# Group statistics, diagonal marks, SiLU and two per-token columns rearranged in an attention and graph-convolution kernel

## The chip, the cores and the metric

The kernel runs on one core of a Trainium2 chip. The metric is device time in microseconds (us) of one execution. A kernel's time is given as the median of several runs; the profile comes from one further execution with its own time.

## The reference, cut to what matters

Input: x, 16 samples of 64 channels by 1024 tokens (32 x 32), f32. The reference applies two residual blocks:

```
y   = gn32(x)                          # 32 groups of 2 channels
q,k = w_q y, w_k y;  v = w_v y         # 4 heads of 32
q   = softmax over 32 dims * scale;  k = softmax over 1024 tokens
o   = w_out(context(k, v) q) + b_out
x1  = x + layernorm over (channels, tokens) of o, with gn_weight, gn_bias

y1  = gn32(x1)
xn  = y1 / ||y1|| per token
sim = xn xn^T (1024 x 1024);  val, idx = top 9 of each row
v   = val / (sum of val + 1e-6)
out = gather-sum(xn w1, idx, v) + b1;   out = silu(groupnorm4(out) gamma1 + beta1)
out = gather-sum(out w2, idx, v) + b2;  out = silu(groupnorm4(out) gamma2 + beta2)
result = x1 + out
```

## The kernel before, in words

A sample is held as 128 partitions by 512 elements: channel c of the first 512 tokens in partition c, of the other 512 in partition 64 + c. Every sample goes through five stages; the samples overlap as in a pipeline.

- `attend`: statistics of x ("in"), y, k and its exp, q with its softmax, the context as a small matrix, `att`.
- `unit`: statistics of att ("at"), x1, statistics of x1 ("mi"), y1, its squares. TensorE sums the squares of each token (L739) into a column of 128 x 8, DVE reads it (L572, L573), POOL raises it to -1/2 (`rn`, L319). The column is needed as a row that is the same in all channels: TensorE transposes it (L743), DVE copies it out (`rnT`, L577), SP stores it in DRAM as 8 rows of 128 (L245), waits for that, and loads it twice with a broadcast (`rbc`, L239). POOL multiplies xn = y1 * rbc (L326). SP copies the two halves of xn crosswise (`xsw`, L255), since TensorE needs both operands in the same partitions.
- `neighbours`: TensorE forms xn w1 (L775) and, for each of 8 blocks of 128 tokens, the similarities to all 1024 (L755) into one of two PSUM tiles `pS`. ACT copies them to `adj` (L444). Then TensorE adds a negative mark on the diagonal of the block (`mark`, L763, f16), so that a token is not among its own eight nearest. DVE finds the 8 largest (L585) and writes a mask with 1.0 in their places (L603). The next product into the same `pS` waits for that mask.
- `weights`: SP transposes each mask by DMA (L263). POOL sets the diagonal of the transposed mask to 1 (L341) and multiplies the mask into `adj` above and left of the diagonal (L347, L337).
- `convolve`: TensorE aggregates (L798, 8 steps of 2 products), DVE multiplies by the weights v (`vbc`, L613), statistics ("g1"), SiLU as half * (1 + tanh): ACT makes `zh` (L450) and the tanh (L464), DVE multiplies (L627). Then the product with w2 (L818), and the same once more ("g2"). The weights v start as a column of 128 x 8 (L588 to L595) and take the same way as rn: transpose L809, copy L634, store L268, two broadcast loads L239.

The statistics of all five tags have one form. DVE makes mean and variance of each partition. TensorE averages the means over the group (`average`, L652, one column), ACT forms the squared deviation (L370) and the negated mean (L372 or L374), TensorE averages variance and squared deviation (`average_sq`, L656, two columns), DVE adds them (L506), POOL makes the power -1/2 (L297), DVE the scale and bias (L511, L516, L518).

Every engine runs its steps in a fixed order. `weave` takes for each stage and sample a list of slot times (`TIMES`), adds the sample's start, and sorts all steps of all samples by that number. The numbers serve for the order alone; what a step waits for is in its semaphores. An engine that waits holds up all that is behind it.

```
live += [(b * PERIOD + at, steps) for at in TIMES[engine][stage.__name__]]
```

Of the kernel before, what the change touches and what calls it, by code (L numbers as in the profile page):

```python
# [24 lines left out]
CONST_PARTS = [("ident", P), ("avg_pair", P), ("avg_sample", P), ("avg_group", P), ("halves", 2)]  # L25
# [6 lines left out]
PERIOD = 41.68  # L32
TIMES = {
    "sync": {
        "attend": [-19.9],
        "unit": [93.77, 96.42, 103.99],
        "neighbours": [114.76, 117.19, 121.63, 128.63, 133.57, 139.3, 144.67, 148.62],
        "convolve": [152.27, 154.92, 243.23],
    },
    "gpsimd": {  # L40
        "attend": [37.93, 64.54],
        "unit": [76.19, 78.34, 83.46, 90.62, 100.3],
        "weights": [121.84, 122.54, 125.69, 126.69, 127.39, 134.58, 135.58, 137.18, 138.48, 140.38, 143.8, 146.0, 150.12,
            152.62, 154.82],
        "convolve": [175.71, 199.3, 212.05],
    },
    "scalar": {
        "attend": [35.3, 41.75, 45.84, 46.44, 50.58, 56.34, 58.34, 70.18, 72.45],
        "unit": [74.74, 77.4, 82.01, 84.5, 85.44],
        "neighbours": [104.23, 109.39, 110.69, 116.84, 119.9, 124.11, 132.94, 136.8, 140.7],  # L50
        "convolve": [174.2, 176.86, 177.68, 180.48, 196.22, 201.2, 204.26],
    },
    "vector": {
        "attend": [0.0, 36.74, 39.73, 45.17, 51.99, 55.51, 56.78, 59.67, 62.39],
        "unit": [73.26, 75.93, 76.86, 79.85, 83.2, 84.24, 90.24, 93.4],
        "tops": [110.91, 112.21, 118.92, 123.25, 126.08, 135.51, 141.79, 144.57, 148.52],
        "masks": [113.39, 115.82, 120.26, 127.26, 132.2, 137.6, 143.3, 147.25],
        "convolve": [151.9, 171.77, 172.55, 175.45, 176.38, 178.6, 191.75, 192.53, 198.02, 200.45, 205.77],
    },
    "tensor": {  # L60
        "attend": [34.51, 36.01, 43.3, 45.14, 48.96, 51.71, 55.24, 59.12, 69.03, 71.3],
        "unit": [74.24, 75.43, 81.51, 82.7, 88.21, 92.89],
        "neighbours": [103.13, 108.19, 109.49, 114.76, 118.37, 121.85, 130.89, 133.57, 139.5],
        "marks": [110.51, 111.81, 118.17, 121.65, 125.57, 134.87, 141.39, 143.72],
        "convolve": [150.87, 157.9, 161.35, 162.44, 165.17, 166.36, 167.45, 169.29, 170.68, 173.7, 174.95, 179.38, 182.18,
            183.27, 184.51, 185.6, 187.39, 188.48, 189.57, 190.66, 195.37, 197.29],
# [12 lines left out]
def shape_constants(C):  # L79
    p = np.arange(P)  # L80
    channel = p % C
    out = {"ident": np.eye(P)}
    for name, size in (("avg_pair", 2), ("avg_sample", C), ("avg_group", C // 4)):
        same = channel[:, None] // size == channel[None, :] // size
        out[name] = same / same.sum(1, keepdims=True)
    out["halves"] = np.arange(P)[:, None] // C == np.arange(2)[None, :]
    return np.concatenate([out[n] for n, _ in CONST_PARTS], axis=1).astype(np.float32)


def build(nc, x, packed, w_vo, out):  # L90
# [11 lines left out]
    with ctx:  # L102
# [12 lines left out]
        halved = sb("halved", [P, 4])  # L115

        def const(name):
# [31 lines left out]
        selfsim = [sb(f"selfsim{i}", [P, NT]) for i in range(2)]  # L149
        rn = sb("rn", [P, NT])  # L150
        rnT = sb("rnT", [NT, P])
        rbc = sb("rbc", [P, H])
        st = {n: sb(f"st_{n}", [P, 16]) for n in ("in", "at", "mi", "g1", "g2")}

# [4 lines left out]
        top = sb("top", [P, NT, TOP])  # L159
        vsum = sb("vsum", [P, NT])  # L160
# [6 lines left out]
        vrT = sb("vrT", [NT, P])  # L167
        vbc = sb("vbc", [P, H])
        g1 = sb("g1", [P, H])
        zh1 = sb("zh1", [P, H])  # L170
        y2 = sb("y2", [P, H])
        g2 = sb("g2", [P, H])
        zh2 = sb("zh2", [P, H])
# [12 lines left out]
            in_stat in_aggr in_mean_ps in_dev in_var_ps in_veps in_rstd in_bias y_ready  # L186
# [673 lines left out]
```

## Time and profile before

| what | value |
|---|---|
| median of 3 runs | 780.92 us (778.73 to 781.6) |
| the profiled execution's own time | 778.75 us |
| its span, first to last instruction | 777.0 us |
| mean granted TensorE clock | 0.921 of 2.4 GHz |
| busy: PE / DVE / POOL / ACT | 663.6 / 574.1 / 483.0 / 353.3 us |
| largest group of TensorE | L798, aggregation, 265.4 us |

1.75 us of the profiled time lie around the span. From about 120 to 690 us one sample is like another; before and after that the pipeline fills and drains. "Busy" of TensorE counts the time in which at least one product is in it.

### The profile page before, as it was taken

The page shows a single profiled execution, that of the slowest core. Times are in us where ns is not written, and L with a number is a line of the kernel's source. Part 1 is how long each engine was busy: PE and PEld are TensorE (multiplying, and loading weights), DVE is VectorE, ACT ScalarE, POOL GpSimd, SP SyncE. Part 2 cuts the span into 40 slices and gives each one's busy share as a digit, 9 for nine tenths or more (in the row PEclk, how much of TensorE's full clock was granted, in tenths as well). Part 3 has the DMA queues.
Part 4 walks back from the last instruction along what each step waited for, and adds up shares of the span by engine and source line. Part 5 has one row for each costly group of instructions (what it writes and reads, how often), then busy time and mean ns, then how long its engine had stood idle before and what let it go on. Part 6 is the DMA issues. An engine that isn't in the chain of part 4 may idle for free.

```text
span 777.0 us, 11257 instructions
## 1 busy us (share of the span) xinstructions
PE 663.6 (85%) x3632; PEld 299.1 (38%) x3632; DVE 574.1 (74%) x1086; ACT 353.3 (45%) x578; POOL 483.0 (62%) x536
## 2 busy tenths in 40 slices
PE   3476869999999999999999999999999999787764
PEld 2353434444343434343434434343434343332221
DVE  2235678888888888888888878888888888866411
ACT  2234436364546555564546454646446454424110
POOL 0122665859596768676776849676767677674600
PEclk9557679999999999999999999999999999988776
DMA  2003242434343442524253434334353424333300
GB/s 68 1 14 56 54 96 54 96 57 95 82 96 68 81 97 56 121 57 109 56 95 68 96 69 96 77 81 88 64 106 64 90 60 83 74 83 75 69 14 14
DMA packets 148731, 55.93 MB, mean 72 GB/s; under 512 B 138017, under 2 KB 138273, under 8 KB 148673
## 3 DMA queue, kind: packets, MB, share of 16 engines
q1 hardware_dynamic: 148672, 55.21, 34.6%
q8 instruction: 29, 0.48, 0.2%
q14 instruction: 30, 0.24, 0.1%
HBM read 13.11 MB, written 4.33 MB: 22 GB/s over the span
## 4 chain that ended last, share of the span: by engine, by line
PE 51%; DVE 18%; issue 16%; POOL 8%; ACT 3%; DMA 2%; SPq 0%; POOLq 0%; ACTq 0%; DVEq 0%
PE pC L798 25%; PE pS L755 9%; DVE mask L603 5%; POOL rn L319 3%; DVE y L627 3%; PE pC L818 2%; PE pB L775 2%; PE pA L673 2%; POOL st_g L297 2%; DVE top L585 2%; PE pA L712 2%; PE pB L701 2%; PE pS L763 2%; ACT pB L464 1%; DVE st_g L497 1%
## 5 line engine op out<-in xcount | busy, mean ns | idle before, releaser
L798 PE MATMUL pC<-adj,xt 128*64 128x512 f32 x1024 | 265.4, 625 | 3.6 <-POOL adj L347 2.8
L585 DVE MAX8 top<-pS 128x8 f32<-128x1024 f32 x128 | 156.8, 1225 | 37.8 <-PE pS L763 36.6
L444 ACT COPY adj<-pS 128x1024 f32<-128x1024 f32 x128 | 129.2, 1009 | 95.1 <-PE pS L755 95.0
L347 POOL TENSOR_TENSOR adj<-maskT,adj 128x128 f32<-128x128 f16 (+7 forms) x128 | 164.4, 1285 | 11.7
L755 PE MATMUL pS<-xn 64*128 64x512 f32 x256 | 153.3, 682 | 10.9 <-DVE mask L603 5.7
L603 DVE MATCH_REPLACE8 mask<-top,pS 128x1024 uint16<-128x1024 f32 x128 | 155.4, 1214 | 0.0
L755 PE MATMUL pS<-xn,xsw 64*128 64x512 f32 x256 | 153.5, 682 | 2.0 <-DVE mask L603 1.8
L337 POOL TENSOR_TENSOR adj<-maskT,adj 128x128 f32<-128x128 f16 (+6 forms) x112 | 130.4, 1165 | 0.0
L798 PEld LDWEIGHTS pC<-adj,xt 128*64 128x64 f32 x1024 | 59.7, 139 | 88.8 <-issue 70.1
L319 POOL TENSOR_TENSOR rn<-ssq,minus_half 128x8 f32<-128x8 f32 x16 | 26.5, 1656 | 49.7 <-DVE selfsim L573 49.7
L613 DVE TENSOR_TENSOR g<-pC,vbc 128x512 f32<-128x512 f32 x32 | 22.1, 692 | 42.5 <-PE pC L798 42.5
L755 PEld LDWEIGHTS pS<-xn 64*128 64x128 f32 x256 | 40.1, 195 | 28.6 <-issue 18.3
L305 POOL TENSOR_TENSOR qn<-qe,qrec 128x1024 f32<-128x1024 f32 x16 | 30.6, 1912 | 30.1 <-DVE qrec L552 30.1
L341 POOL TENSOR_SCALAR_AFFINE_SELECT maskT<-maskT 128x128 f16<-128x128 f16 x128 | 37.7, 295 | 17.8 <-DMA maskT<-mask 17.7
L297 POOL TENSOR_TENSOR st_at<-st_at,minus_half 128x1 f32<-128x1 f32 x16 | 8.7, 542 | 59.3 <-DVE st_at L506 59.3
L755 PEld LDWEIGHTS pS<-xn,xsw 64*128 64x128 f32 x256 | 40.0, 195 | 7.0 <-DVE mask L603 3.5
L763 PEld LDWEIGHTS pS<-mark,place 64*128 64x128 f16 x256 | 14.6, 95 | 72.9 <-issue 36.6
L818 PE MATMUL pC<-w,y 128*128 128x128 f32 x128 | 21.1, 315 | 24.8 <-DVE y L627 24.8
L297 POOL TENSOR_TENSOR st_g<-st_g,minus_half 128x1 f32<-128x1 f32 x32 | 17.4, 543 | 38.9 <-DVE st_g L506 38.9
L370 ACT ACTIVATE st_g<-pC,st_g 128x1 f32<-128x1 f32 x32 | 8.4, 264 | 63.2 <-PE pC L652 63.2
L314 POOL TENSOR_TENSOR x<-attn,xs 128x512 f32<-128x512 f32 x16 | 20.4, 1274 | 23.7 <-ACT attn L420 23.7
L437 ACT COPY xt<-pB 128x512 f32<-128x512 f32 x16 | 9.4, 586 | 56.6 <-PE pB L775 56.6
(120 smaller groups left out, 1035.2 us busy)
## 6 DMA issues: line engine op xcount, KB each, us to landing
xs<-x SPq DMA_DIRECT2D x32, 128.0 KB, 2.8
rbc<-rn_row SPq DMA_DIRECT2D x32, 128.0 KB, 2.9
xsw<-xn SPq DMA_DIRECT2D x32, 128.0 KB, 2.5
vbc<-v_row SPq DMA_DIRECT2D x32, 128.0 KB, 2.9
out<-res SPq DMA_DIRECT2D x32, 128.0 KB, 2.4
maskT<-mask SPq DMA_TRANSPOSE x128, 3.1
cst<-packed SPq DMA_DIRECT2D x1, 453.5 KB, 3.5
rn_row<-rnT SPq DMA_DIRECT2D x16, 4.0 KB
```

The source lines that it names most:

```text
L297: pool.tensor_tensor(st[tag][:, 13:14], st[tag][:, 12:13], minus_half[:, 0:1], ALU.pow).then_inc(done[f"{tag}_rstd"], 1)
L305: pool.tensor_tensor(qn[:, :, :], qe[:, :, :], qrec[:, :].unsqueeze(2).broadcast_to([P, NT * HEADS, D]), ALU.mult).then_inc(done["q_norm"], 1)
L319: pool.tensor_tensor(rn[:, :], ssq[:, :], minus_half[:, :], ALU.pow).then_inc(done["rn_ready"], 1)
L337: pool.tensor_tensor(left, m[:, 0:r, r, :].bitcast(F16), left, ALU.mult).then_inc(done["lower"], 1)
L341: pool.affine_select(out=own, in_=own, compare_op=ALU.not_equal, fill=1.0, base=0, pattern=[[-1, P]], channel_multiplier=1).then_inc(done[ ...
L347: pool.tensor_tensor(above, m[:, r, 0:r + 1, :].bitcast(F16), above, ALU.mult).then_inc(done["upper"], 1)
L444: act.copy(adj[b % 2][:, r, :], pS[r % 2][:, :]).then_inc(done["sim_copied"], 1)
L585: dve.max(top[:, r, :], pS[r % 2][:, :]).then_inc(done["tile_top"], 1)
L603: dve.match_replace(out=mask[n % MASKS][:, :], in_to_replace=top[:, r, :], in_values=pS[r % 2][:, :], imm_value=ONE_BITS).then_inc(done["t ...
L755: mm = pe.matmul(pS[r % 2][:, h * H:(h + 1) * H], src[b % 2][c, rows], xn[b % 2][c, :], start=True, stop=True)
L798: mm = pe.matmul(pC[h * C:(h + 1) * C, :], xt[:, t % NJ, t // NJ, :], adj[b % 2][:, t, h * H:(h + 1) * H], start=(t == 0), stop=(t == NT - 1))
L818: mm = pe.matmul(pC[:, j * P:(j + 1) * P], y2[:, j * P:(j + 1) * P], w2[:, :], start=True, stop=True)
```

## The change

What it does, part by part:

1. Statistics: one TensorE product per statistic in place of two. ACT first spreads the mean of each partition over as many columns as the group has partitions (`spread`: 4, 128 or 32 columns, by a constant that picks), TensorE averages these columns, the mean and the variance in one product, and ACT squares and sums the deviations from the columns (`accum_out`). The shift by b1 or b2 moves from DVE to ACT.
2. Marks: they are added in the same step as the similarities. ACT's copy then holds marked similarities; DVE's maximum waits for that copy. The diagonal of `adj`, zero after the mask, gets the token's similarity to itself by a sum: ACT makes `selves` (8 per sample, a diagonal matrix of 128 x 128), POOL adds it (`diagonal`), in place of L341.
3. SiLU: one ACT instruction with the function Silu in place of two on ACT (one with Tanh) and one on DVE.
4. Sums: the similarity to itself and the 1e-6 stand beside the eight largest in `top` (now two buffers), so that one reduction replaces L588 and L591.
5. Columns: rn and v go from SBUF to DRAM element by element, without a transpose by TensorE and without a copy by DVE. The store has 1024 elements of 4 bytes in place of 8 rows of 512.
6. The slot lists of all engines are new, and each sample has a start of its own.

```diff
+            def spread(b, tag, pick, shift=None):
+                n = channels[tag]
+                mean = spread_mean[tag][:, n:n + 1]
+                act.wait_ge(*of(f"{tag}_aggr", b))
+                if shift is not None:
+                    act.activation(mean, mean, ACT.Identity, bias=shift).then_inc(done[f"{tag}_shift"], 1)
+                    act.wait_ge(*of(f"{tag}_shift", b))
+                act.activation(spread_mean[tag][:, 0:n], pick, ACT.Copy, scale=mean).then_inc(done[f"{tag}_spread"], 1)
...
+                act.activation(st[tag][:, 10:11], ps[:, n:n + 1], ACT.Copy, scale=-n ** -0.5).then_inc(done[f"{tag}_minus"], 1)
+                if DEVIATIONS[tag] == 2:
+                    act.activation(st[tag][:, 9:10], ps[:, n:n + 1], ACT.Identity if shift is not None else ACT.Copy,
+                                   bias=0.0 if shift is None else shift, scale=-1.0).then_inc(done[f"{tag}_dev"], 1)
+                act.activation(apart[tag][:, :], ps[:, 0:n], ACT.Square, bias=st[tag][:, 10:11], scale=n ** 0.5,
+                               accum_out=st[tag][:, 8:9]).then_inc(done[f"{tag}_dev"], 1)
...
-            def average(b, tag, ps, avg, signal):
-                pe.matmul(ps[:, 0:1], const(avg), st[tag][:, 6:7], start=True, stop=True).then_inc(done[f"{tag}_mean_ps"], 1)
-            def average_sq(b, tag, ps, avg):
-                pe.matmul(ps[:, 1:3], const(avg), st[tag][:, 7:9], start=True, stop=True).then_inc(done[f"{tag}_var_ps"], 1)
+            def average(b, tag, ps, avg):
+                n = channels[tag]
+                pe.wait_ge(*of(f"{tag}_spread", b))
+                pe.matmul(ps[:, 0:n + 2], const(avg), spread_mean[tag][:, :], start=True, stop=True).then_inc(done[f"{tag}_mean_ps"], 1)
...
-                sp.wait_ge(*of("rnT_copied", b))
-                sp.dma_start(rn_row[b, :, :], rnT[:, :]).then_inc(done["rn_saved"], 16)
+                sp.wait_ge(*of("rn_ready", b))
+                sp.dma_start(rn_row[b, :, :].rearrange("t p -> p t"), rn[:, :], allow_slow_non_contiguous=True).then_inc(done["rn_saved"], 16)
...
-                sp.wait_ge(*of("vT_copied", b))
-                sp.dma_start(v_row[b, :, :], vrT[:, :]).then_inc(done["v_saved"], 16)
+                sp.wait_ge(*of("v_rec", b))
+                sp.dma_start(v_row[b, :, :].rearrange("t p -> p t"), vrec[b % 2][:, :], allow_slow_non_contiguous=True).then_inc(done["v_saved"], 16)
...
-                    pool.affine_select(out=own, in_=own, compare_op=ALU.not_equal, fill=1.0, base=0, pattern=[[-1, P]],
-                                       channel_multiplier=1).then_inc(done["diagonal"], 1)
+                    pool.wait_ge(*of_tile("upper", n))
+                    pool.wait_ge(*of_tile("self_ready", n))
+                    own = a[:, r, r * P:(r + 1) * P]
+                    pool.tensor_tensor(own, own, selves[:, r, :], ALU.add).then_inc(done["diagonal"], 1)
...
+            def itself(b):
+                for r in range(NT):
+                    yield
+                    act.wait_ge(*of("ss_read", b, 2))
+                    act.wait_ge(*of_tile("diagonal", NT * (b - 1) + r))
+                    act.activation(selves[:, r, :], ident, ACT.Copy, scale=top[b % 2][:, r, TOP:TOP + 1]).then_inc(done["self_ready"], 1)
...
+                act.activation(dst[:, :], src[:, :], ACT.Silu, bias=st[tag][:, 15:16], scale=st[tag][:, 14:15]).then_inc(done[signal], 1)
...
-                    dve.wait_ge(*of_tile("marked", n))
-                    dve.wait_ge(*of("v_sum", b - 1))
-                    dve.max(top[:, r, :], pS[r % 2][:, :]).then_inc(done["tile_top"], 1)
+                    dve.wait_ge(*of_tile("sim_copied", n))
+                    dve.wait_ge(*of("v_tot", b - 2))
+                    dve.max(top[b % 2][:, r, 0:TOP], pS[r % 2][:, :]).then_inc(done["tile_top"], 1)
```

Orders that the text below speaks of. TensorE, from the sum of squares (L739) to the first similarity product of the same sample, before: similarity block 5 of the sample before, mean of g1, transposes of ek, deviation of g1, block 6, transpose of rn, a mark, q, the product with w2, ky (L701), block 7, and then seven aggregation steps with the small product m (L706), three marks and xn w1 (L775). After: transposes of ek, the one average of g1, block 6, q, block 7, ky, the product with w2, m, five aggregation steps, xn w1. SP, around the store of rn, is the same in both: mask transpose 4 of the sample before, store of rn, the two loads, mask transpose 5; the crosswise copies come before transpose 6 in the new order, behind it in the old. DVE reads the sum of squares behind the read of g1 and its statistics in both. ACT's functions in one period of the new order: Exp (of k), then other functions, Silu, Silu, copies, Exp (of q).

## Rows read from the trace of the kernel before

**Rows 1.** Windows: busy of each engine in one period, clock, DMA share, GB/s

```profile
core 0: us, PE busy (x) PEld busy (x) DVE busy (x) ACT busy (x) POOL busy (x), PEclk, DMA share, GB/s
400.00:441.68 41.68, 39.00 (x228) 17.25 (x226) 35.67 (x68) 21.91 (x37) 30.15 (x34) 1.00 0.42 83
```

**Rows 2.** The page, part 4: the chain that ended last, by engine

```profile
PE 51%; DVE 18%; issue 16%; POOL 8%; ACT 3%; DMA 2%; SPq 0%; POOLq 0%; ACTq 0%; DVEq 0%
```

**Rows 3.** Timeline of TensorE, 398 to 442 us (start, length, idle before and releaser)

```profile
398.35 0.69 PE L755 MATMUL pS<-xn 64*128 64x512 f32 x1
...
402.95 1.08 PE L719 MATMUL pB<-qh,mT 128*64 128x512 f32 x4 [0.55 <-ACT qh L408]
...
412.83 0.38 PE L652 MATMUL pB<-st_mi,cst 128*128 128x1 f32 x2 [0.28 <-DVE y L627]
...
420.31 1.05 PE L739 MATMUL pB<-cst,sq 128*128 128x2 f32 x8
...
422.37 0.38 PE L652 MATMUL pC<-st_g,cst 128*128 128x1 f32 x2
422.62 1.07 PE L684 MATMUL pA<-cst,ek 128*128 128x128 f32 x8
...
424.79 0.27 PE L743 MATMUL pB<-cst,rn 128*8 128x128 f32 x1
425.00 0.23 PE L763 MATMUL pS<-mark,place 64*128 64x64 f16 x2
...
427.56 1.16 PE L818 MATMUL pC<-w,y 128*128 128x128 f32 x8 [1.24 <-DVE y L627]
...
435.34 1.16 PE L775 MATMUL pB<-w,xn 128*128 128x128 f32 x8
...
440.01 0.69 PE L755 MATMUL pS<-xn 64*128 64x512 f32 x1
```

**Rows 4.** Chain of waits in order of time (start, time in the chain, what)

```profile
428.72 1.02 PE pB L701 x16
429.75 1.06 PE pS L755 x4
430.80 1.01 PE pC L798 x4
...
432.98 0.25 PE pB L706 x8
```

**Rows 5.** Groups by line and shape, whole span (busy us, mean ns, idle before)

```profile
L341 POOL TENSOR_SCALAR_AFFINE_SELECT maskT<-maskT 128x128 f16<-128x128 f16 x128 | 37.7, 295 | 17.8 <-DMA maskT<-mask 17.7
...
L464 ACT ACTIVATE pB<-g,st_g 128x512 f32<-128x512 f32 x32 | 24.7, 772 | 0.0
...
L627 DVE SCALAR_TENSOR_TENSOR y<-pB,zh 128x512 f32<-128x512 f32 x32 | 21.9, 684 | 8.1 <-ACT pB L464 8.1
...
L337 POOL TENSOR_TENSOR adj<-maskT,adj 128x128 f32<-128x128 f16 x16 | 6.9, 430 | 0.0
...
L364 ACT ACT_TABLE_LOAD x1 | 1.3, 1283 | 0.7 <-PEq L854 0.7
```

**Rows 6.** Timeline of POOL, 398 to 442 us

```profile
422.54 1.66 POOL L319 TENSOR_TENSOR rn<-ssq,minus_half 128x8 f32<-128x8 f32 x1 [2.99 <-DVE selfsim L573]
...
431.43 1.28 POOL L326 TENSOR_TENSOR xn<-y,rbc 128x512 f32<-128x512 f32 x1
```

**Rows 7.** Timeline of SP, 424 to 442 us

```profile
425.48 0.28 SPq L245 DMA_DIRECT2D rn_row<-rnT  x1
426.91 1.11 SPq L239 DMA_DIRECT2D rbc<-rn_row  x2
...
436.14 1.18 SPq L255 DMA_DIRECT2D xsw<-xn  x2
```

**Rows 8.** The page, part 6: DMA issues, KB each, median us to landing

```profile
rbc<-rn_row SPq DMA_DIRECT2D x32, 128.0 KB, 2.9
xsw<-xn SPq DMA_DIRECT2D x32, 128.0 KB, 2.5
```

**Rows 9.** The tile maskT: landing of the 128 mask transposes

```profile
DMA to landing us min/median/max: 3.0/3.1/4.9
```

More of the change, by code:

```diff
@@ L85, in shape_constants @@
         out[name] = same / same.sum(1, keepdims=True)
+    for name, size in (("pick_pair", 2), ("pick_group", C // 4)):
+        out[name] = (p // C * size + channel % size)[:, None] == np.arange(2 * size)[None, :]
     out["halves"] = np.arange(P)[:, None] // C == np.arange(2)[None, :]
@@ L158, in build @@
         maskT = [sb(f"maskT{i}", [P, NT, NT, P], U16) for i in range(2)]
-        top = sb("top", [P, NT, TOP])
-        vsum = sb("vsum", [P, NT])
+        top = [sb(f"top{i}", [P, NT, TOP + 2]) for i in range(2)]
+        selves = sb("selves", [P, NT, P])
         vtot = sb("vtot", [P, NT])
@@ L218, in weave @@
                     next(steps)
-                    live += [(b * PERIOD + at, steps) for at in TIMES[engine][stage.__name__]]
+                    live += [(BEGINS[b] + at, steps) for at in TIMES[engine][stage.__name__]]
             for _, steps in sorted(live, key=lambda e: e[0]):
@@ L289, in _ @@
             pool.memset(minus_half[:, :], -0.5).then_inc(done["prepared"], 1)
+            for p in range(2):
+                pool.memset(top[p][:, :, TOP + 1:TOP + 2], 1e-6 * SSCALE).then_inc(done["prepared"], 1)
             pool.memset(w1[:, :], 0.0).then_inc(done["prepared"], 1)
@@ L415, in unit @@
                 yield
+                spread(b, "at", ident)
+                yield
                 deviation(b, "at", pB)
@@ L421, in unit @@
                                scale=st["at"][:, 14:15]).then_inc(done["at_normed"], 1)
+                yield
+                spread(b, "mi", const("pick_pair"))
                 yield
@@ L475, in convolve @@
                 yield
[L476 to L479 removed]
+                spread(b, "g2", const("pick_group"), const("b2"))
+                yield
+                deviation(b, "g2", pB, const("b2"))
+                yield from silu(b, "g2", g2, y3, "y3_ready")
+            weave("scalar", attend, unit, itself, neighbours, convolve)
         @block.vector
@@ L681, in attend @@
                 yield
+                pe.wait_ge(*of("k_exp", b))
                 pe.wait_ge(*of("k_exp", b))
@@ L779, in neighbours @@
                     similarity(b, r)
-            def marks(b):
-                for r in range(NT):
-                    yield
-                    mark(b, r)
             def aggregate(b, xt, signal):
@@ L821, in convolve @@
                 yield
-                pe.wait_ge(*of("vT_copied", b + 1))
-                average(b, "g2", pC, "avg_group", "g2_mean")
-                yield
-                average_sq(b, "g2", pC, "avg_group")
-            weave("tensor", attend, unit, neighbours, marks, convolve)
+                if b < 13:
+                    pe.wait_ge(*of("att_copied", b + 3))
+                elif b < 14:
+                    pe.wait_ge(*of("xt1_copied", b + 2))
+                else:
+                    pe.wait_ge(*of("g1_veps", b))
+                average(b, "g2", pB, "avg_group")
+            weave("tensor", attend, unit, neighbours, convolve)
 def kernel(**inputs):
```

278 lines of the change are left out of this document (123 added, 155 removed).

## The prediction, made before the changed kernel was run

> **What bounds the kernel now.** I read the busy time by windows first. In the stretch where samples follow each other evenly, TensorE is busy 39.00 us in a window of 41.68, DVE 35.67, POOL 30.15 and ACT 21.91, at the full clock of 2.4 GHz [rows 1]. The timeline of TensorE then gives the period: the first similarity product comes at 398.35 and again at 440.01, so one sample takes 41.66 us, and 15 such distances are 625 of the 777 us of the span [rows 3]. TensorE works 39.0 of each period and idles 2.66. The reader should see that the idle time is a few named waits: 0.55 for qh, 1.24 for the activated y2 ahead of the product with w2, 0.28 for y3 ahead of an average [rows 3]; 0.59 is left for shorter ones. The chain of waits agrees: TensorE has 51% of it, the rest is spread [rows 2]. So a TensorE slot that goes is worth its length in every period, and a wait anywhere else is worth only what it makes TensorE wait.
>
> **Statistics.** Ten small products per sample become five. A product of one column holds TensorE from 422.37 to 422.62, 0.25 us, where the next work is ready, and shows 0.38 where it is not [rows 3]; I take 0.3. The new ones have 6, 34 or 130 columns. The nearest row for the widest is the product of 128 columns: four take 1.16 us, 0.29 each [rows 3], so width costs nothing, and five products go: 5 x 0.3 = 1.5 us. Against it, the average now waits for ACT's spread, a step more than before; in return a whole turn between ACT and TensorE is gone. I charge 0.2 per period for averages that come later because ACT is in its own order.
>
> **Columns on TensorE.** The transpose of rn holds TensorE from 424.79 to 425.00, 0.21 us [rows 3], that of v is the same product: 0.4 us go. TensorE's work falls from 39.0 to 39.0 - 1.5 - 0.4 = 37.1 us.
>
> **Marks.** The same 8 pairs stay, so no work goes. They no longer wait for ACT's copy, and DVE's maximum starts one turn through TensorE sooner. I count nothing: what hides it is that TensorE has other work between the blocks. If that cover were gone, the similarity products would wait on masks.
>
> **POOL, DVE, ACT.** POOL exchanges 8 x 0.295 for 8 sums of 128 x 128, nearest row 0.430 [rows 5]: 30.1 + 1.1 = 31.2 us. DVE loses two multiplications of 0.684 [rows 5], two copies and some small ones of 0.2 to 0.7, about 3 us: 32.7. ACT loses two Tanh of 0.772 [rows 5] and gains five spreads, eight diagonal matrices and some nine small ones; at 0.2 to 0.3 each that is 5 to 6 us, so ACT stands at about 26. None reaches 37.1; all are priced at nothing while each stays off TensorE's waits. y2 comes sooner: 0.772 and 0.684 fall out of its chain [rows 5].
>
> **Function tables.** The profile has one table load in the whole span, of 1283 ns [rows 5]. If Silu and Exp cannot be in the tables together, the order Exp, Silu, Silu, Exp needs two loads per sample, 2.6 us of ACT, which then has 28.7 of 40. I take them as hidden: the first can run while ACT waits for the bias of g1. If the cover is gone, each adds up to 1.3 us ahead of y2 or of q's exp. The Trainium skill, ScalarE: Activation LUTs, section on what ACT_TABLE_LOAD costs, puts a switch at about 2.66 us with its drain, and by it two exposed switches would take 5.3 us per sample and make the kernel slower; its 1283 ns for the load agree with the row, and no row here shows a drain.
>
> **The columns' way through DRAM.** This is the unknown cost. Today the store of rn is issued at 425.48 and the load that waits for it at 426.91, so 1.43 us for 8 rows [rows 7]. The new store has 1024 packets, 64 for each of 16 engines. Call the extra x. Lower end: 0, if elements cost nothing. The nearest row is the mask transpose, also 1024 small packets: it lands in 3.1 us, at most 4.9 [rows 9]. So x = 3.1 - 1.4 = 1.7, upper end 3.5. The chain from the end of the sum of squares to the first similarity product, by rows: 420.31 + 1.05 = 421.36 to rn at 422.54 is 1.2 (DVE's order ahead of it is the same); rn 1.66 [rows 6]; store 1.43 + x; the two loads, the second issued 0.55 after the first and landing in 2.9 [rows 7, 8], 3.45; xn 1.28 [rows 6]; the crosswise copies, the second 0.6 later and landing in 2.5 [rows 7, 8], 3.1; four semaphore turns of 0.1. That is 12.5 + x = 14.2 us. Today TensorE reaches that product 440.01 - 421.36 = 18.65 us after the sum, so the chain is covered, and the copies even wait until 436.14 behind a mask transpose [rows 6, 7]. In the new order TensorE has less in between: transposes of ek 1.02, the average 0.3, two blocks of 1.06 with marks of 0.16, q and ky 1.02 each, w2 1.1, m 0.25, five steps of 1.01, xn w1 1.09 [rows 3, 4]: 13.3 us. So a wait of 0.9 us appears ahead of the first block. The wait of 1.24 ahead of w2 lies in the same stretch and shortens, since y2 comes sooner and 4.5 us of work stand between the average and w2. The two do not add: I keep 1.24 for the stretch. What queues behind SP's wait for the store is mask transpose 5, the two copies and the next transposes; x = 1.7 there is less than a mask's place in its ring of three. The column of v has over 15 us until it is used, so x is hidden there.
>
> The Trainium skill, DMA: Bandwidth & Descriptors, rules for kernel authors, speaks against this part: a strided last dimension becomes one descriptor per element, and a rearranged pattern is said to be 19 times slower than the hardware transpose. No row here shows such a store; rival B is the mechanism that this rule names.
>
> **The sum.** Period: work 37.1; waits 2.66 less the 0.28 for y3 (the new wait there is for an earlier signal), 2.4; ACT's order 0.2: 39.7 us. Fifteen periods: 15 x (39.7 - 41.66) = -29.4 us. The ends of the pipeline: filling, the column takes x longer but loses a product and a copy, for two or three samples; draining, SiLU is shorter by 1.4 four times and the v column longer: 0, give or take 5. Against the profiled execution: 778.75 - 29.4 = 749.4. The median of the runs stands 2.2 above that execution, so 751.5 us.
>
> **Rivals.**
> *A, the gain is cut by ACT.* Two table loads and eight diagonal matrices stand in ACT's queue ahead of y2 or qh. For it: ACT's part in the chain is in-order, and qh already holds TensorE up 0.55 [rows 3]. Against: ACT idles 20 us of a period. One exposed load of 1.3 us: period 41.0, 778.75 - 10 + 2 = 771 us. Chance 0.13.
> *B, the element store becomes the bound (slower).* Period = 37.1 + 1.1 (the other waits) + 12.5 + x - 13.3, which is 37.4 + x. It passes 41.66 at x = 4.3, somewhat above the longest transpose. At x = 6 the period is 43.4, so 780.9 + 26 = 807 us. For it: a packet of 4 bytes written to DRAM is in no row, and SP waits for it with mask transpose 5 behind. Against: 1024 packets of 256 bytes land in 3.1. Chance 0.12. By the Trainium skill (same page and section) the store would take, as an estimate, 19 x 3.1 = 59 us, and the time would be a multiple of the present one; no row bears that size out.
> *C, nothing on TensorE binds after all*: the masks' path through DVE, SP and POOL keeps 41.66 and the work taken away becomes idle time. 781 us. For it: DVE's 35.67. Against: it falls to 32.7. The case also holds that the parts cancel. Chance 0.07.
> *D, more than forecast:* x near 0 and y2 early, waits of 1.3: period 38.4, 732 us. Chance 0.08.
>
> **How the numbers follow.** The forecast (x from 1 to 3.5 gives periods of 39 to 41, 742 to 770) has 0.60, and its likeliest point is 751.5. D's, B's and part of C's chance stay outside: the range is 741 to 776, which takes in A. A measurement of this kernel tells about 0.5% from no change, 777 to 785. Faster by more than that: forecast 0.60, A 0.13, D 0.08, together 0.81; within it C, 0.07; slower: B, 0.12.
>
> **What would show it.** Right: a period of 39.7 us; TensorE busy 37.1 in it; average products of 0.3 whatever their width; idle ahead of L818 under 1.2 and a new wait of about 1 us ahead of a sample's first block, released by the crosswise copy; the loads of rbc 3.1 us after the store. ACT_TABLE_LOAD twice per sample, beside idle time. Wrong: a store that lands after 6 us, with TensorE waiting on xn w1 or the first block for more than 3 us per period; table loads that y2 waits for; the clock below 1.00 in the even stretch.

## The result and the profile after

The changed kernel takes 865.69 us (median of 4 runs, 862.48 to 867.53), the kernel before 780.34 in the same session: a ratio of 1.109, interval 1.105 to 1.113. It is slower by 85 us, where 751.5 had been forecast. The profiled execution has a span of 865.7 us at a mean granted clock of 0.851 of 2.4 GHz.

The page first: busy time by engine, and the chain that ended last by engine and line (against [rows 2]).

```profile
PE 651.1 (75%) x3440; PEld 324.3 (37%) x3440; DVE 527.4 (61%) x970; ACT 450.2 (52%) x941; POOL 504.4 (58%) x538
...
issue 33%; POOL 22%; PE 19%; DMA 12%; ACT 7%; DVE 5%; SPq 1%; POOLq 0%; ACTq 0%; DVEq 0%
DMA rn_row<-rn 9%; PE pS L773 7%; POOL adj L351 6%; PE pC L804 5%; POOL adj L346 4%; POOL rn L328 3%; PE pB L787 3%; ACT adj L481 2%; POOL xn L335 2%; PE pA L727 2%; POOL adj L357 2%; POOL x L322 2%; DMA v_row<-vrec 1%; ACT selves L468 1%; 
```

No engine is the bound any more. TensorE had 51% of the chain [rows 2] and has 19%; at the head of the lines stands a transfer, the store of rn. The windows view of one period of the mean length (columns as in [rows 1]) says the same:

```profile
403.57:450.97 47.40, 37.06 (x210) 17.74 (x208) 32.70 (x60) 28.32 (x59) 30.11 (x34) 0.90 0.50 72
```

TensorE works 37.06 of 47.40 us, part of it at a lower clock (0.90 in the mean), and idles 10.3, where it idled 2.66 of 41.66 [rows 1, 3]. The table of waits names who holds up whom (sum over the run, times, longest); first the engines, then SP's queue:

```profile
POOL xn L335 <- issue: 136.2, 15, 9.9
...
PE pB L787 <- POOL xn L335: 104.8, 16, 10.7
```

```profile
SPq L245 <- DMA rn_row<-rn: 133.0, 13, 11.5
...
SPq L245 <- DMA v_row<-vrec: 63.0, 14, 11.4
```

Read from the bottom of the chain up: SP waits for its own store of rn, POOL waits for the broadcast rbc behind it ("issue" here is the landing of the two loads, which that view does not name), TensorE waits for xn. The timelines of one sample show it in time. POOL and SP:

```profile
432.94 1.65 POOL L328 TENSOR_TENSOR rn<-ssq,minus_half 128x8 f32<-128x8 f32 x1
...
449.66 1.26 POOL L335 TENSOR_TENSOR xn<-y,rbc 128x512 f32<-128x512 f32 x1 [9.73 <-issue]
```

```profile
434.62 0.40 SPq L251 DMA_DIRECT2D rn_row<-rn  x1
445.84 1.09 SPq L245 DMA_DIRECT2D rbc<-rn_row  x2
...
450.95 1.15 SPq L261 DMA_DIRECT2D xsw<-xn  x2
```

And TensorE:

```profile
402.19 2.08 PE L787 MATMUL pB<-w,xn 128*128 128x128 f32 x8 [6.76 <-POOL xn L335]
405.24 1.19 PE L773 MATMUL pS<-xn 64*128 64x512 f32 x1 [0.98 <-issue]
...
417.67 0.46 PE L664 MATMUL pB<-spread_at,cst 128*128 128x130 f32 x2 [0.16 <-ACT spread_at L384]
...
429.99 1.05 PE L760 MATMUL pB<-cst,sq 128*128 128x2 f32 x8
...
436.99 1.16 PE L823 MATMUL pC<-w,y 128*128 128x128 f32 x8 [0.48 <-ACT y L490]
...
438.91 4.51 PE L804 MATMUL pC<-adj,xt 128*64 128x512 f32 x20 [0.52 <-ACT xt L501]
450.97 2.08 PE L787 MATMUL pB<-w,xn 128*128 128x128 f32 x8 [7.55 <-POOL xn L335]
454.02 1.19 PE L773 MATMUL pS<-xn 64*128 64x512 f32 x1 [0.97 <-issue]
```

From the store (434.62) to the loads that wait for it (445.84) 11.2 us pass in this sample; over 14 samples it is 9.15 to 11.98, 10.28 in the mean, where the 8 rows took 1.43 [rows 7]. TensorE has finished its aggregation at 443.4 and stands still for 7.55 us. After that pause xn w1 takes 2.08 in place of 1.16 [rows 3]: the granted clock is at its lower level, 1.2 GHz, for that product (windows of 450.97 to 453.05 and of 454 to 456 show 0.50) and the first two similarity blocks, which hold TensorE from 454.02 to 457.93, 3.9 us where two blocks with their marks took 2.2 at full clock.

### The profile page after: what moved, and what is told of

Its sections match the earlier page's. It is cut to its first block, busy times and chain, and to the rows that moved or that the text cites. A ratio compares the mean times of both kernels' runs of the same rounds, so it can differ in the third digit from the quotient of the medians.

```text
span 865.7 us, 11490 instructions
## 1 busy us (share of the span) xinstructions
PE 651.1 (75%) x3440; PEld 324.3 (37%) x3440; DVE 527.4 (61%) x970; ACT 450.2 (52%) x941; POOL 504.4 (58%) x538
## 2 busy tenths in 40 slices
DMA packets 181502, 55.97 MB, mean 65 GB/s; under 512 B 171040, under 2 KB 171040, under 8 KB 181440
## 4 chain that ended last, share of the span: by engine, by line
issue 33%; POOL 22%; PE 19%; DMA 12%; ACT 7%; DVE 5%; SPq 1%; POOLq 0%; ACTq 0%; DVEq 0%
DMA rn_row<-rn 9%; PE pS L773 7%; POOL adj L351 6%; PE pC L804 5%; POOL adj L346 4%; POOL rn L328 3%; PE pB L787 3%; ACT adj L481 2%; POOL xn L335 2%; PE pA L727 2%; POOL adj L357 2%; POOL x L322 2%; DMA v_row<-vrec 1%; ACT selves L468 1%; POOL st_at L305 1%
## 5 line engine op out<-in xcount | busy, mean ns | idle before, releaser
L804 PE MATMUL pC<-adj,xt 128*64 128x512 f32 x1024 | 248.8, 621 | 9.0 <-ACT xt L501 9.0
L773 PE MATMUL pS<-xn 64*128 64x512 f32 x256 | 175.0, 775 | 18.6 <-issue 16.9
L773 PE MATMUL pS<-xn,xsw 64*128 64x512 f32 x256 | 173.6, 778 | 3.3 <-DVE mask L625 3.3
L804 PEld LDWEIGHTS pC<-adj,xt 128*64 128x64 f32 x1024 | 72.2, 142 | 119.2 <-issue 116.1
L787 PE MATMUL pB<-w,xn 128*128 128x128 f32 x128 | 31.9, 428 | 104.8 <-POOL xn L335 104.8
L335 POOL TENSOR_TENSOR xn<-y,rbc 128x512 f32<-128x512 f32 x16 | 20.2, 1261 | 151.2 <-issue 136.2
L787 PEld LDWEIGHTS pB<-w,xn 128*128 128x128 f32 x128 | 27.3, 315 | 117.5 <-POOL xn L335 117.5
L357 POOL TENSOR_TENSOR adj<-adj,selves 128x128 f32<-128x128 f32 x128 | 58.2, 455 | 9.5 <-ACT selves L468 0.6
L775 PEld LDWEIGHTS pS<-mark,place 64*128 64x128 f16 x256 | 27.9, 109 | 86.2 <-issue 86.2
L468 ACT ACTIVATE selves<-cst,top 128x128 f32<-128x128 f32 x128 | 42.1, 390 | 0.0
```

Source lines behind the costliest of these rows:

```text
L335: pool.tensor_tensor(xn[b % 2][:, :], y1[:, :], rbc[:, :], ALU.mult).then_inc(done["xn_ready"], 1)
L357: pool.tensor_tensor(own, own, selves[:, r, :], ALU.add).then_inc(done["diagonal"], 1)
L468: act.activation(selves[:, r, :], ident, ACT.Copy, scale=top[b % 2][:, r, TOP:TOP + 1]).then_inc(done["self_ready"], 1)
L773: pe.matmul(pS[r % 2][:, h * H:(h + 1) * H], src[b % 2][c, rows], xn[b % 2][c, :], start=True, stop=True)
L787: mm = pe.matmul(pB[:, j * P:(j + 1) * P], xn[b % 2][:, j * P:(j + 1) * P], w1[:, :], start=True, stop=True)
L804: mm = pe.matmul(pC[h * C:(h + 1) * C, :], xt[:, t % NJ, t // NJ, :], adj[b % 2][:, t, h * H:(h + 1) * H], start=(t == 0), stop=(t == NT - 1))
```

## The experiments

The kernel before was timed beside each group, with medians from 780.5 to 780.8 us. "Period" is the mean distance of one sample's loads of rbc from the next one's, "store to loads" the mean time from the issue of the store of rn to that of the first load that waits for it; both over 14 samples, without the first and the last. By this count the kernel before has a period of 41.8 us.

### One column back in rows, then both

From the changed kernel, rn goes through TensorE and DVE again; the second kernel does it for v as well (the same edit with vrT):

```diff
-                sp.dma_start(rn_row[b, :, :].rearrange("t p -> p t"), rn[:, :], ...)
+                sp.dma_start(rn_row[b, :, :], rnT[:, :]).then_inc(done["rn_saved"], 16)
+                dve.tensor_copy(rnT[:, :], pC[0:NT, 0:P]).then_inc(done["rnT_copied"], 1)
+                pe.transpose(pC[0:NT, 0:P], rn[:, :], ident).then_inc(done["rn_T"], 1)
```

> The changed kernel, but rn goes to DRAM as 8 rows again (transpose by TensorE into pC, copy by DVE, slots added behind the sixth similarity block); v stays by element. Theory S (the element store of rn, 11.2 us from its issue to the loads behind it, is what made the kernel slower; all else is as forecast): period 39.7 to 40.5 us, 750 to 765 us, no wait of TensorE over 2 us ahead of xn w1. Rival R (ACT's longer queue with two table loads, or the new order, costs it too): above 790 us with store gone. Rival V (v by element holds SP as well, 11.4 us at most): 765 to 800, and the kernel with both columns by rows clearly below this one.

> As the one before, and v too goes as 8 rows through a transpose and a copy. TensorE has 37.5 us of work per period. Theory S: 750 to 765 us, within 5 us of the kernel with rn alone by rows. Rival V: 15 us or more faster than that kernel. Rival R: above 790 us.

Measured: 718.52 us (714.16 to 722.09), ratio 0.920 (0.914 to 0.926), and 720.32 us, ratio 0.923. One store of 4 KB per sample is worth 147 us of 866. Both kernels are 30 us faster than expected, so "all else is as forecast" does not hold; the other parts are taken up further down. The second kernel shows no gain over the first: v by element costs nothing that can be told. TensorE in the first one, and SP's store and loads:

```profile
399.97 0.27 PE L770 MATMUL pC<-cst,rn 128*8 128x128 f32 x1
...
403.27 1.16 PE L834 MATMUL pC<-w,y 128*128 128x128 f32 x8
...
405.19 4.51 PE L814 MATMUL pC<-adj,xt 128*64 128x512 f32 x20 [0.52 <-ACT xt L502]
409.63 1.16 PE L796 MATMUL pB<-w,xn 128*128 128x128 f32 x8
...
437.32 0.27 PE L770 MATMUL pC<-cst,rn 128*8 128x128 f32 x1
```

```profile
400.58 0.28 SPq L252 DMA_DIRECT2D rn_row<-rnT  x1
402.06 1.09 SPq L246 DMA_DIRECT2D rbc<-rn_row  x2
```

xn w1 follows the aggregation without a pause and at full clock. From transpose to transpose 37.35 us pass, in an undisturbed sample; the periods run from 36.0 to 41.6, 38.3 in the mean. Windows of that sample:

```profile
399.97:437.32 37.35, 35.41 (x219) 17.27 (x215) 32.80 (x62) 28.27 (x59) 31.49 (x34) 1.00 0.57 97
```

### The same edits put into the old kernel

From the kernel before, one column at a time goes by element (the transpose and the copy go, waits on them move to what they stood for); nothing else is changed.

> The kernel before with one part of the change: rn is stored by element, its transpose and copy go. Theory S: the store takes 11.2 us where 1.4 were; the old order covers 18.65 us from the sum of squares to the first block, the chain is 12.5 + 9.8 - 0.7 = 21.6, so TensorE waits 3 us more per period and loses 0.2: 44.5 us, 778.75 + 42 = 821 us; more if the mask transposes behind SP's wait are late too (up to 47.4 as in the changed kernel, 865). A rival that the store is slow only beside the other edits: under 790 us.

> The kernel before with v stored by element, its transpose and copy gone. Theory S with cover: v is used 15 us after its load is issued in the old order, so the extra 10 us are hidden and TensorE saves 0.2 per period: 775 to 782 us. Rival: SP waits 11 us for the store with the first mask transposes of the next sample behind it, and masks come late: 790 to 830 us.

Measured: rn by element 882.98 us, ratio 1.133 (1.128 to 1.138), store to loads 9.09, period 48.3. So the element store makes either order slow, the old one by 102 us, the new one by 147. The size is a miss (821 us expected, 865 at most): between 120 and 600 us TensorE idles 7.8 us per period, 5.1 more than before, where 3 more had been expected, and after the pause xn w1 takes 2.08 us here too. v by element 777.55 us, ratio 0.996 (0.993 to 0.998), although SP waits for it much longer than the 13.7 us of before (table of waits, SP's queue):

```profile
SPq L238 <- DMA v_row<-vrec: 128.6, 16, 8.7
```

A slow store is harmless where nobody needs its data for 15 us, and what TensorE saves by it is 0.2 us per sample.

### What makes the store slow

All start from the changed kernel. Where the elements go elsewhere, the broadcast loads read a row of x in place of rn, as the expectations say; the wait of SP for its store stays.

```diff
# half of the elements
+                sp.dma_start(rn_row[b, 0:NJ, :].rearrange("t p -> p t"), rn[:, 0:NJ], ...)
# 512, 64, 8 and 4 bytes apart: W = 128, 16, 2, 1; loads of x
+        rn_wide = nc.dram_tensor("rn_wide", (B, NT, P, W), F32, kind="Internal").ap()
+                sp.dma_start(rn_wide[b, :, :, 0].rearrange("t p -> p t"), rn[:, :], ...)
# to SBUF, 8 bytes apart; loads of x
+                sp.dma_start(rnx[:, :, 0], rn[:, :], ...)
# even and odd partitions in two stores
+                for o in range(2):
+                    sp.dma_start(rn_row[b, :, o:P:2].rearrange("t p -> p t"), rn[o:P:2, :], ...)
```

> The changed kernel, but only 4 of the 8 columns of rn are stored, 512 elements, and both halves of the tokens take these norms (the norms of the other half are left out). In the changed kernel the loads were issued 9.2 to 12.0 us after the store, 10.4 in the mean, against 1.4 for 8 rows. Theory P (a price per element: 9.0 us over 64 elements of each engine, 0.14 us each): 1.4 + 4.5 = 5.9 us from store to loads, 4.5 us less per period, about 800 us. Rival F (a fixed cost of such a store): it stays over 9 us and the time over 855 us.

> The changed kernel, but the 1024 elements of rn go to DRAM 512 bytes apart, each into a line of its own, and the loads of rbc read a row of x instead (the norms are left out of xn). Theory P: the packets are as many, so 9 to 12 us from store to loads and 855 to 880 us. Rival L (neighbouring elements share a line of DRAM, and their writes wait for each other): under 6 us from store to loads, and under 810 us.

> The changed kernel, but the 1024 elements of rn are copied by DMA into SBUF, 8 bytes apart in the same partitions, and the loads of rbc read a row of x instead (the norms are left out of xn). If 4-byte packets are slow wherever they go (theory P): 9 to 12 us from the copy to the loads, 855 to 880 us. Rival W (the writes into DRAM are what is slow): 2 to 4 us, as the mask transposes with their 1024 packets into SBUF, and under 760 us.

> As the kernel with elements 512 bytes apart, but 8 bytes apart, so that each stretch of 512 bytes of DRAM gets half as many writes as in the changed kernel. There the loads came 10.3 us after the store, with half the rows stored still 9.4, with 512 bytes between elements 2.9. If writes into one stretch of DRAM queue up one behind the other, (10.3 - 2.9) / 2 goes: 6.0 to 7.0 us from store to loads, and 790 to 825 us. If the price hung on the number of packets: 10 us as before. If only direct neighbours disturb each other: near 3 us.

> As the kernel with elements 512 bytes apart, but 64 bytes apart. If the price is one of sharing 64 bytes or less: 2.9 us from store to loads as with 512, 730 to 742 us. If stretches of 512 bytes count: between 2.9 and 4.5 us.

> As the kernel with elements 512 bytes apart, loads of rbc from a row of x, but the elements side by side as in the changed kernel. If the distance makes the price: 9 to 12 us from store to loads, and 850 to 880 us. If reading the stored rows back makes it: 3 to 4.5 us, and 730 to 745 us.

> The changed kernel, but rn is stored by two DMAs, even and odd partitions, one issued behind the other without a wait; rows and loads as in the changed kernel. If only direct neighbours within one DMA disturb each other: 5 to 6 us from the first store to the loads, 750 to 780 us. If every write into the same bytes of DRAM's lines counts, whoever makes it: 9 to 13 us and 850 to 890 us.

| store of rn | store to loads, us | period, us | median, us | ratio |
|---|---|---|---|---|
| 8 rows of 512 bytes (one column back in rows) | 1.43 | 38.3 | 718.5 | 0.920 |
| 1024 elements, side by side (the change) | 10.28 | 47.6 | 865.7 | 1.109 |
| the same, loads of x (control) | 9.77 | 46.7 | 847.9 | 1.087 |
| the same, in two stores | 9.60 | 46.3 | 842.0 | 1.079 |
| 512 elements, side by side | 9.20 | 46.5 | 846.2 | 1.084 |
| 1024 elements, 8 bytes apart | 4.53 | 39.8 | 738.7 | 0.946 |
| 64 bytes apart | 2.71 | 40.4 | 747.8 | 0.958 |
| 512 bytes apart | 2.93 | 39.8 | 734.4 | 0.941 |
| into SBUF, 8 bytes apart | 2.66 | 40.4 | 747.5 | 0.958 |

Apart from the first two rows, each kernel has two runs. The kernels with fewer elements, with loads of x or with the copy into SBUF leave the norms out and serve for their times alone.

SP's timeline with 512 bytes, then the control with 4 bytes from one element to the next:

```profile
411.83 0.39 SPq L251 DMA_DIRECT2D rn_wide<-rn  x1
415.47 1.11 SPq L256 DMA_DIRECT2D rbc<-x  x2
...
424.61 0.58 SPq L274 DMA_DIRECT2D v_row<-vrec  x1
...
436.41 1.59 SPq L245 DMA_DIRECT2D vbc<-v_row  x2
```

```profile
423.46 0.40 SPq L251 DMA_DIRECT2D rn_wide<-rn  x1
434.80 1.11 SPq L256 DMA_DIRECT2D rbc<-x  x2
```

The two kernels differ by one number, the distance of the elements in DRAM. The store of v is a second control, within the kernel with 512 bytes: it still has its elements side by side, and its loads come 11.8 us after it in the timeline, 11.7 in the mean.

It is not the count of elements or of packets: half of the elements save 1.1 us of 10.3, and all of them, further apart, come to 2.9 with the same 181502 packets in the whole profile. (The half leaves out whole rows, so a stored element has the same neighbours as before.) It is not that the loads read what was just written, for the control reads x and stays slow. Nor is it the time of the DMA engines: by the rows of single packets in the trace, nearly all packets of 4 bytes are done on average 1.7 us after the store's issue, side by side as with 512 bytes, but the sixteen signals that the store has landed come on average from 8.4 us on in one case and from 2.1 on in the other.

It is writes of 4 bytes lying side by side in DRAM; 8 bytes of distance already take away most. No run wrote side by side into SBUF, so the row on SBUF compares with 8 bytes in DRAM (4.53), not with the changed kernel.

Two stores of every second partition, whose elements are 8 bytes apart within each store, are no faster than one. Both are in flight together, since the packets of both are done after 2.3 us. But their landing signals come in two groups: the sixteenth of the 32 on average 5.5 us after the first issue, the seventeenth after 8.1, the last after 9.7. So one store, presumably the first, lands about as soon as one with 8 bytes of distance alone (4.5), and only the other is late. Whether that one pays for neighbours that the first has just written, or for standing behind it, these runs do not separate. How the memory handles such neighbours was not found out; that they are merged into a larger unit of the memory one after another is only argued.

Several of these expectations missed. The kernel with 8 bytes was expected at 6.0 to 7.0 us and over 790, or near 3, and fell between; so neither "half the writes, half the price" nor "direct neighbours alone" is right as it stands. The side-by-side kernels were expected over 850 us and took 842 to 848, that with 64 bytes under 742 and took 748. Below 5 us the time no longer follows the store: 2.66 gives 747.5, 4.53 gives 738.7. The two runs with 512 bytes are 9 us apart, so little can be made of the 13 us between these kernels; they stay unexplained.

### What the other parts give

All but the last start from the kernel with rn back in rows, since only there can the rest be seen.

```diff
# marks behind ACT's copy: the products of L784 as a step of their own
+                pe.wait_ge(*of_tile("sim_copied", n))
+                mm.then_inc(done["marked"], 1)
# tanh again
-                act.activation(dst[:, :], src[:, :], ACT.Silu, ...)
+                act.activation(zh[tag][:, :], src[:, :], ACT.Identity, ...)
+                act.activation(dst[:, :], src[:, :], ACT.Tanh, ...)
+                dve.scalar_tensor_tensor(out=act_out[:, :], in0=act_out[:, :], scalar=1.0, in1=zh[tag][:, :], op0=ALU.add, op1=ALU.mult)
# averages twice
+                pe.matmul(ps[:, 0:n + 2], const(avg), spread_mean[tag][:, :], start=True, stop=True)
# the kernel before, marks joined with the similarities
-                    dve.wait_ge(*of_tile("marked", n))
+                    dve.wait_ge(*of_tile("sim_copied", n))
```

> The kernel with rn by rows (718.5 us), but the marks are again products of their own that wait for ACT's copy, and DVE's maximum waits for them; slots for them behind the next steps. If joining marks and similarities saves TensorE about 0.1 us per block (a block with its mark took 1.11 us against 1.06 + 0.16) and a turn in the path of the masks: 37.35 + 0.8 to 1.6 per period, 730 to 745 us. If the marks gave nothing, as I forecast: 715 to 722 us. The order has not been made for late marks, so a result over 750 us would speak of the order, not of the marks.

> The kernel with rn by rows (718.5 us), but SiLU again as half * (1 + tanh): two ACT instructions in place of one, a DVE product behind them, no table loads. If the table loads of that kernel are hidden (the trace has one at 434.60, ending with the bias that Silu waits for) and SiLU's shorter chain is worth what the wait ahead of the product with w2 was (1.24 us per period before, 0 in most periods now): 1 to 2 us more per period, 733 to 750 us. If the table loads cost TensorE time (rival A of the prediction), they go here, and the kernel is no slower or is faster: 700 to 720 us.

> The kernel with rn by rows, but each of the five average products is done twice into the same place. By my term of 0.3 us each and TensorE as the bound: 5 x 0.3 x 16 = 24 us more, 742 us. If TensorE is not the bound (rival C): under 725 us.

> The kernel before with one part of the change: the marks come right behind the similarities of their block and before ACT's copy, DVE's maximum waits for the copy, the slots of the marks are empty; the diagonal of adj keeps the marked similarity (the sum with the token's own similarity is left out). My forecast gave this part nothing: 775 to 782 us. If it is what the sum missed (0.1 us of TensorE's time per block, and masks that come sooner): 755 to 772 us.

**Marks behind the copy** in the new order: 817.87 us, ratio 1.050. This run tells little. The places of the eight marks were put into the order by hand, and the waits show that they fell badly (table of waits):

```profile
DVE top L616 <- PE pS L791: 158.4, 51, 7.5
```

It is a miss: it prices a bad order. The clean form is the last edit, **marks joined in the old kernel**, where they move into steps that are there already: 760.64 us, ratio 0.974 (0.972 to 0.976), 20 us less, period 40.8. TensorE's timeline there:

```profile
404.06 0.69 PE L755 MATMUL pS<-xn 64*128 64x512 f32 x1
...
405.02 0.22 PE L757 MATMUL pS<-mark,place 64*128 64x64 f16 x2
405.17 0.38 PE L656 MATMUL pB<-st_in,cst 128*128 128x2 f32 x2
```

A block with its mark holds TensorE for 1.11 us (404.06 to 405.17), where a block took 1.06 and a mark 0.16 by themselves. Eight times 0.11 is 0.9 us of the period, most of the 1.0 gained. The forecast had been no change; the other value of the expectation, 755 to 772 us, holds. The groups by line show where the time went. The marks' own group hardly changes (29.5 to 28.7 us); the aggregation's falls from 265.4 to 253.3 us. Marks no longer stand between its steps:

```profile
L787 PE MATMUL pC<-adj,xt 128*64 128x512 f32 x1024 | 253.3, 616 | 1.2 <-ACT xt L474 0.8 <-DVE st_g L506 0.4
```

**Tanh again**: 753.01 us, ratio 0.966 (0.961 to 0.970), so Silu is worth 34 us in this order (the expectation, 733 to 750, was a little short). TensorE's waits with Tanh, with Silu, and in the kernel before (three tables of waits):

```profile
PE pB L682 <- ACT spread_g L387: 25.6, 27, 3.7
PE pC L847 <- DVE y L660: 23.0, 15, 4.4
```

```profile
PE pB L669 <- ACT spread_g L385: 23.1, 26, 2.5
...
PE pC L834 <- ACT y L491: 4.8, 3, 3.0
```

```profile
PE pC L818 <- DVE y L627: 24.8, 16, 3.7
```

The wait ahead of the product with w2 stands in 15 samples without Silu and in three with it: 18 us. Another 7 lie in the draining, 94.6 us behind the last loads of rbc where it is 87.4 with Silu. DVE's additional step was put into the order by hand, so the rest, 9 us, stays open. The two table loads are there (27 in the changed kernel behind the one at the start, with two groups of 1283 ns each), and ACT's timeline with rn in rows shows what they cost:

```profile
401.10 1.28 ACT L491 ACT_TABLE_LOAD   x1
402.40 1.52 ACT L491 ACTIVATE y<-g,st_g 128x512 f32<-128x512 f32 x2
...
405.98 1.28 ACT L431 ACT_TABLE_LOAD   x1
407.27 1.06 ACT L431 ACTIVATE qe<-qs 128x1024 f32<-128x1024 f32 x1
```

The first load ends 0.5 us after the bias that Silu waits for (DVE's last step for it ends at 401.87), but y2 is there just as TensorE reaches L834 (403.27 above, no wait); the product behind the softmax of q starts at 412.83, without a wait too. So here the loads are hidden from TensorE. No run took the loads away and left Silu.

**Averages twice**: 734.22 us, ratio 0.938 (0.934 to 0.942), 14 to 16 us for 80 more products: about 0.2 us for each, by the two intervals 0.1 to 0.25, and not the 0.3 of the forecast. The groups of the second products have the same length with 130 columns as with 6:

```profile
L670 PE MATMUL pB<-spread_at,cst 128*128 128x130 f32 x32 | 6.4, 284 | 0.0
L670 PE MATMUL pB<-spread_mi,cst 128*128 128x6 f32 x32 | 6.3, 267 | 0.0
```

## Why the prediction was wrong

**The step that failed is the size of x.** The sum took the element store's extra time as x = 1.7, upper end 3.5, from the mask transposes, because they too are 1024 small packets [rows 9]. Measured, x = 10.28 - 1.43 = 8.9. The row was the wrong kin: its packets have 256 bytes and go into SBUF. The run into SBUF lands in 2.3 and costs 2.66, close to those 3.1; so the row did price small packets, but not writes side by side in DRAM, and "the nearest row, however far" was no bound. The upper end should have been open. **Rival B had the mechanism**, and its own formula gives 37.4 + 8.9 = 46.3 us; measured are 47.6. The remaining 1.3 per period lies in TensorE's busy time, and goes with the clock. The windows view of the changed kernel and of the one with rn in rows:

```profile
120.00:600.00 480.00, 385.56 (x2134) 191.78 (x2132) 325.00 (x594) 281.65 (x584) 313.24 (x329) 0.89 0.45 71
```

```profile
120.00:600.00 480.00, 447.97 (x2700) 219.23 (x2701) 410.76 (x761) 354.57 (x739) 392.75 (x415) 0.99 0.53 88
```

That is 38.2 us busy and 9.4 idle per period in the changed kernel. B counts 37.1 and 9.2. With rn in rows TensorE is busy 35.7, so the lower clock costs about 2.7 (0.99 in xn w1, 1.7 in the two blocks), and B comes this close partly by luck, since its 37.1 of work was too much by 1.6. In time: 778.75 + 15 x (46.3 - 41.66) = 848, measured 866. B's bound of x = 4.3 cannot be read off the runs so sharply, but x = 3.1 (8 bytes apart) is still fast and x = 7.8 (half of the elements) is slow.

The Trainium skill's rule that spoke against this part (DMA: Bandwidth & Descriptors, Rules for kernel authors) pointed the right way. Its factor of 19 gave an estimate of 59 us; the store took 10.3, and as many elements into SBUF 2.7. The measurement decides: the price depends on where the elements lie, which the rule doesn't speak of.

**With x as forecast, the period would have been right, but by errors that cancel, and the time not.** With elements 512 bytes apart, x is 2.93 - 1.43 = 1.5 and the period 39.8 against 39.7 forecast. In it TensorE is busy 36.4 us and idle 3.4 (439.29 us busy of 480), where 37.1 and 2.6 were forecast. The time is 734 against 751.5, under the range's lower end of 741. What is missing are the ends of the pipeline, priced at 0, give or take 5: the time ahead of the first loads of rbc and behind the last is 153.6 us before, 143.0 there and 144.8 with rn in rows. The parts, from the kernel with rn in rows:

- *TensorE's work, 37.1.* Measured 35.4 in the undisturbed sample (with one transpose of two still there). Averages: forecast 1.5 less. The groups by line have eight groups of L652 and L656 before, 62.9 us together, and four after, 33.1; first and last of each:

```profile
L652 PE MATMUL pC<-st_g,cst 128*128 128x1 f32 x64 | 12.2, 260 | 6.0 <-DVE st_g L502 5.0 <-DVE vrT L634 1.0
...
L656 PE MATMUL pB<-st_at,cst 128*128 128x2 f32 x32 | 6.3, 268 | 0.8 <-ACT st_at L372 0.8
```

```profile
L814 PE MATMUL pC<-adj,xt 128*64 128x512 f32 x1024 | 247.4, 618 | 12.2 <-ACT xt L502 9.0 <-POOL adj L358 3.2
...
L669 PE MATMUL pB<-spread_g,cst 128*128 128x34 f32 x64 | 12.6, 280 | 23.6 <-ACT spread_g L385 23.1
...
L669 PE MATMUL pB<-spread_mi,cst 128*128 128x6 f32 x32 | 6.4, 270 | 1.2 <-ACT spread_mi L385 1.2
```

  That is (62.9 - 33.1) / 16 = 1.9 per sample, while doubling the products gave 0.2 for each, 1.0 for five: 1.5 lies between, and width cost next to nothing, as said (7.7 us against 6.4 for 16 products that stand alone). Not in the sum were the marks (0.9) and the aggregation, L814 above: 247.4 us for the same 1024 products that took 265.4 at L798, 1.1 less per sample. The two are not separate terms: the marks joined in the old kernel already bring the aggregation to 253.3, 0.8 less per sample. In the new order the steps stand in rows of three and five (five in 4.51 us above, 0.90 each) where a step alone holds TensorE for 1.01 [rows 4]. That the order does the rest is read off these rows; no run changed the order alone. A part that a diff calls "slot lists are new" can have a price too.
- *Marks, priced at 0.* Wrong by 20 us in the old order. The cover named, TensorE's other work between the blocks, hides a wait; what went was TensorE's own time. "The same 8 pairs stay, so no work goes" took work for what is issued, not for how long it holds the engine.
- *Silu.* "I keep 1.24 for the stretch" was the second large error: 34 us. The wait ahead of w2 was one of DVE's and ACT's chain, that chain became 1.4 us shorter, and the wait all but went. That wait is 18 of the 34 us, about what 1.24 per period makes. The table loads were hidden from TensorE, as forecast; rival A (771 us) did not come. By the Trainium skill's rule (ScalarE: Activation LUTs, What ACT_TABLE_LOAD costs) it would have been up to 5.3 us per sample if both switches were exposed. Its 1283 ns are in the rows, its drain is not: in the changed kernel a load starts at 434.60, 0.02 us after ACT's copy ends, and with rn in rows the activation starts 0.02 us behind the load (401.10 + 1.28 to 402.40).
- *ACT's order, 0.2.* Too small: TensorE waits 23.1 us for spread_g over the run, about 1.5 a sample, where the old mean of that group waited 5.0 and the deviation 3.0. In the undisturbed sample all waits are 1.94, against 2.66 before and 2.6 forecast.
- *v hidden.* Right, in both orders: its loads come 8.9 us after its store in the old order and 10.8 in the new with rn in rows, against the 15 available.
- *POOL 31.2, DVE 32.7, ACT 28.7.* Measured 31.5, 32.8 and 28.3 in the undisturbed sample: right.

So rivals C and D: nothing of C; D (732 us, "y2 early, waits of 1.3") had the direction of the rest of the change, which with rn in rows gives 62 us less than before. Singly measured, in different orders, marks 20, Silu 34 and five averages fewer (16 x 5 x 0.2 = 16) make 70; they needn't add up, and the waits for spread_g stand against them.

The signs named beforehand were the right ones to look for: a store landing after 6 us, TensorE waiting on xn w1 for more than 3 us, the clock below 1.00. All three are in the profile.

**The version that beats both** is the change without its element store of rn: 718.5 us, 8.0% under the kernel before (interval 7.4 to 8.6%) and 17% under the changed one. Whether v goes by element or in rows makes no difference that can be told.

## What to carry to other kernels

A transposed store to DRAM of single 4-byte elements side by side is to be priced as its own thing, about 10 us of latency for 4 KB here, and belongs only where its data is not needed for that long; on a chain with 13 us of cover, a TensorE transpose, a copy and 8 rows are far cheaper. When the trace has no row of the same kind, with the same destination and the same layout, the price has no upper end, and one look at that single operation is worth more than any nearest row. When several edits come together, cost the reordering as well: aggregation products that followed their own kind were shorter, and a chain made shorter can take its whole wait with it, not a part.

## What was not expected of the hardware

- 1024 elements of 4 bytes take 9.8 to 10.3 us from store to waiting load when they lie side by side in DRAM, 4.5 at 8 bytes, 2.7 at 64 and 2.9 at 512; 512 of them side by side still take 9.2. Two stores of every second partition don't help (9.6).
- Nearly all packets of such a store are done after 1.7 us, whatever the distance; the landing signals come from 8.4 us on side by side, from 2.1 on with 512 bytes. The price does not show as busy DMA engines.
- The same element count into SBUF, 8 bytes apart, takes 2.7, where 8 rows into DRAM take 1.4.
- A table load of 1283 ns follows the instruction before it and is followed by the activation at once, with no drain between them in the trace.
- An average of 130 columns costs TensorE about 0.2 us behind another product, like one of 6.
- After the pause of 7 to 8 us TensorE's xn w1 and the two blocks behind it run at 1.2 GHz (2.08 us for 1.16): work that is read at full clock gets longer by a new wait ahead of it.
